# Regrouping a feature-major tile into pairs by way of DRAM, with eight key batches beside it and two linear maps multiplied into one

## What is computed

```python
def _encoder_block(x, Wq, bq, Wk, bk, Wv, bv, Wo, bo, rel_bias, W1, b1, W2, b2):
    q = x @ Wq.T + bq;  k = x @ Wk.T + bk;  v = x @ Wv.T + bv
    qm = q.reshape(d_batch * NB_HEADS, q_len, d_head)      # k and v likewise
    att = jax.nn.softmax(jnp.einsum('nqd,nkd->nqk', qm, km), axis=-1)
    ...                                                    # batch_pos from rel_bias
    att_out = jnp.einsum('nqk,nkd->nqd', att + batch_pos, vm)
    att_out = att_out.reshape(d_batch, q_len, d) @ Wo.T + bo
    att_block = layer_normalize(att_out + x)
    ff = (att_block @ W1.T + b1) @ W2.T + b2
    return layer_normalize(ff + att_block)
```

## Time and profile before

| | |
|---|---|
| median of 3 runs | 1202.9 us (1199.35 to 1207.03) |
| the profiled execution | 1196.92 us |
| its span, first to last instruction | 1195.0 us |
| mean granted TensorE clock | 0.964 of full speed |
| PE, DVE, ACT, POOL busy | 92%, 57%, 48%, 30% of the span |

### The profile page before, as it was taken

The page is one execution under the profiler, slowest core; times in us unless marked ns, Lnnn a source line. Parts: engine busy times, 40 slices in busy tenths (PEclk is TensorE's granted clock), DMA queues, the critical chain, the costliest instruction groups (busy, mean ns, idle before and its releaser), DMA issues.

```text
span 1195.0 us, 26831 instructions
## 1 busy us (share of the span) xinstructions
PE 1099.0 (92%) x9273; PEld 756.1 (63%) x9273; DVE 681.1 (57%) x2035; ACT 577.4 (48%) x1279; POOL 353.6 (30%) x554
## 2 busy tenths in 40 slices
PE   7879998999998899999988668899999999999987
PEld 4455666878776467566655446477777776666554
DVE  5575446455555564778865466533334334688774
ACT  5552224443343554677764133343534344678665
POOL 2217002112111304355440071040404040466561
PEclk9979999999999989999999759799999999999989
DMA  8700120122231003355540301011111211100000
GB/s 260 257 0 27 40 71 22 47 56 58 53 55 50 1 2 115 90 166 165 157 155 1 53 24 47 0 54 53 51 56 44 63 40 58 49 2 2 2 2 19
DMA packets 64859, 73.75 MB, mean 62 GB/s; under 512 B 5936, under 2 KB 57408, under 8 KB 64392
## 3 DMA queue, kind: packets, MB, share of 16 engines
q1 hardware_dynamic: 61496, 64.14, 19.5%
q0 software_dynamic: 1376, 7.49, 1.9%
q10 hardware_dynamic: 1904, 0.98, 0.5%
HBM read 69.98 MB, written 0.52 MB: 59 GB/s over the span
## 4 chain that ended last, share of the span: by engine, by line
PE 81%; DVE 7%; ACT 5%; DMA 3%; issue 2%; POOL 1%; ACTq 1%; SPq 0%; DVEq 0%; POOLq 0%
PE PS L544 14%; PE PS L556 13%; PE PS L1175 7%; PE PS L1186 6%; PE PS L831 5%; PE PS L795 4%; PE PS L547 3%; PE PS L838 2%; PE PS L1207 2%; PE PS L782 2%; PE PS L1164 2%; ACT XN L1419 2%; DMA AR<-AR 1%; PE PS L1157 1%; ACT AR L1419 1%
## 5 line engine op out<-in xcount | busy, mean ns | idle before, releaser
L556 PEld LDWEIGHTS PS<-WB,AR 128*128 128x128 f32 x1504 | 182.3, 192 | 42.8 <-issue 38.6
L556 PE MATMUL PS<-WB,AR 128*128 128x128 f32 x1504 | 182.9, 275 | 0.1
L1419 ACT ACTIVATE AR<-PS,WB 128x512 f32<-128x512 f32 x160 | 110.0, 687 | 148.8 <-PE PS L544 141.0
L2047 DVE SCALAR_TENSOR_TENSOR ACC<-PS,SM,ACC 128x128 f32<-128x128 f32 x192 | 54.1, 344 | 95.9 <-PE PS L556 94.5
L1922 DVE TENSOR_TENSOR AR<-PS,AR 128x512 f32<-128x512 f32 (+2 forms) x71 | 49.8, 701 | 92.4 <-issue 38.6
L544 PE MATMUL PS<-ZT,WB 128*128 128x512 f32 x208 | 100.5, 606 | 0.2 <-DMA WB<-in_units 0.2
L1175 PE MATMUL PS<-AR 64*128 64x257 f32 x512 | 90.5, 429 | 1.0 <-POOL AR L2882 1.0
L544 PE MATMUL PS<-XNT,WB 128*128 128x512 f32 x168 | 87.6, 628 | 0.6 <-DMA WB<-in_units 0.6
L1419 ACT ACTIVATE AR<-PS 128x512 f32<-128x512 f32 (+2 forms) x83 | 43.8, 528 | 85.2 <-PE PS L547 70.1
L1186 PE MATMUL PS<-W,AR 128*128 128x128 f32 x512 | 80.1, 282 | 1.3 <-ACT AR L1419 1.3
L2824 POOL TENSOR_TENSOR AR<-AR,SM 128x516 f32<-128x516 f32 x32 | 33.7, 1054 | 155.5 <-ACT SM L1419 93.8
(11 more groups left out here) (340 smaller groups left out, 2130.9 us busy)
## 6 DMA issues: line engine op xcount, KB each, us to landing
WB<-in_units SPq DMA_DIRECT2D x49, 385.0 KB, 3.1
CTX<-in_fside SPq DMA_DIRECT2D x32, 514.0 KB, 3.9
CTX<-in_ctxT SPq DMA_DIRECT2D x72, 130.0 KB, 2.1
CTX<-in_ctxN SPq DMA_DIRECT2D x32, 129.0 KB, 2.3
CTX<-in_ctxN SPq DMA_DIRECT2D x4, 516.0 KB, 7.0
AR<-in_ctxN SPq DMA_DIRECT2D x4, 516.0 KB, 10.6
AR<-in_ctxN SPq DMA_DIRECT2D x32, 64.5 KB, 3.1
AR<-in_l1x_w POOLq DMA_DIRECT2D x1, 2048.0 KB, 7.9
```

The lines of the kernel that those rows point to most:

```text
L556: m = pe.matmul(PS[:, 4 + hh, 128 * t:128 * t + 128], f_h[hh][:, c, 128 * t:128 * t + 128], WB[:, q, 2 * UNIT + 128 * c:2 * UNIT + 128 * c ...
L1419: return act.activation(o, i, fn, **k)
L2047: ins = dve.scalar_tensor_tensor(out=a, in0=y, scalar=f_w[:, 4 * hh + t, bass.ds(e, 1)], in1=a, op0=ALU.mult, op1=ALU.add)
```

## The change

The three tiles q, k and v are staged separately. Each is written to a DRAM buffer in its new partition order, as one DMA of 128 x 16 pieces of 64 elements (256 bytes), and read back as one DMA of 128 rows of 4 KB. All six DMAs are issued by SP. Queries and keys are waited for by `pair_landed`, values by `pair_v`.

`kv_early` has 8 batches in place of 12. The other 16 are divided: 10 before the output projection, 2 behind it and 4 behind the second map, where the six `keep_clock` matmuls are gone. ACT takes both keys and values of the last four.

After the landing POOL writes two of the four masked copies of the second half and ACT the other two; POOL's copies of v are gone, since PE reads v where it landed. PE does the first scores before it turns v. ACT runs exp(u+1) ahead of copy(u).

`W1` and `W2` are multiplied during `kv_early`, with `b1 @ W2` added to `b2`, and the sequence map, eviction, map becomes one map by the product, written over `l2a_w1`.

```diff
 LIVE = 8
+KV_EARLY = 8
...
+        dram = nc.dram_tensor("pair_dram", (3, P, TOK), F32, kind="Internal").ap()
+        pair_dram = [dram[k] for k in range(3)]
...
+        kv_order = [20 + n for n in range(12)] + [LIVE + n for n in range(12)]
...
-        c_v = ar(10240, TOK)
-        c_tokens = ar(2048, 3072)
-        c_pairs = ar(14336, 3072)
-        staged = lambda k: c_tokens.rearrange("p (u k x) -> p k u x", u=H, k=3)[:, k]
-        pair_part = lambda k: c_pairs.rearrange("p (c k m) -> p k m c", c=H, k=3)[:, k]
-
-        def to_pairs(u):
-
-
-            return (c_pairs[DK * u:DK * u + DK, :].rearrange("i (c y) -> i c y", c=H),
-                    c_tokens[:, 192 * u:192 * u + 192])
+        c_wide = ar(1024, P)
+        c_w1 = ar(1024 + P, P)
+        c_tokens = [ar(a, TOK) for a in (2048, 3072, 6144)]
+        c_pairs = [ar(14336 + TOK * k, TOK) for k in range(3)]
+        pair_part = lambda k: c_pairs[k].rearrange("p (c m) -> p m c", c=H)
+
+        def sent(k):
+
+            return (pair_dram[k].rearrange("(u i) (c x) -> (i c) u x", u=H, c=H),
+                    c_tokens[k].rearrange("p (u x) -> p u x", u=H))
+
+        def to_pairs(k):
+
+            return c_pairs[k], pair_dram[k]
...
+            sp.wait_ge(sig["pair_staged"], 1)
+            sp.dma_start(*sent(0)).then_inc(sig["pair_sent"], 16)
+            sp.wait_ge(sig["pair_staged_d"], 1)
+            sp.dma_start(*sent(1)).then_inc(sig["pair_sent_k"], 16)
+            sp.wait_ge(sig["pair_sent"], 16)
+            sp.dma_start(*to_pairs(0)).then_inc(sig["pair_landed"], 16)
             sp.wait_ge(sig["pair_staged"], 2)
-            sp.wait_ge(sig["pair_staged_d"], 1)
-            for u in range(1, H, 2):
-                sp.dma_start(*to_pairs(u)).then_inc(sig["pair_landed"], 16)
-            sp.wait_ge(sig["pair_landed"], 16 * H)
-            sp.wait_ge(sig["kv_ready"], 24)
+            sp.dma_start(*sent(2)).then_inc(sig["pair_sent"], 16)
+            sp.wait_ge(sig["pair_sent_k"], 16)
+            sp.dma_start(*to_pairs(1)).then_inc(sig["pair_landed"], 16)
+            sp.wait_ge(sig["pair_sent"], 32)
+            sp.dma_start(*to_pairs(2)).then_inc(sig["pair_v"], 16)
+            sp.wait_ge(sig["pair_landed"], 32)
+            sp.wait_ge(sig["pair_v"], 16)
+            sp.wait_ge(sig["kv_ready"], 2 * KV_EARLY)
...
-                pe.matmul(bank(k), VW[:, v, :], source, start=True, stop=True).then_inc(sig["cv_ready"], 1)
+                to = bank(k).rearrange("p (m c) -> p m c", c=H) if len(source.shape) == 3 else bank(k)
+                pe.matmul(to, VW[:, v, :], source, start=True, stop=True).then_inc(sig["cv_ready"], 1)
...
                 pe.wait_ge(sig["keys_landed0"], 32)
-                for n in range(12):
+                for n in range(KV_EARLY):
                     if n == 0:
                         pe.wait_ge(sig["pair_staged"], 1)
                     elif n == 1:
                         pe.wait_ge(sig["pair_staged_d"], 1)
+                        pe.transpose(PS[:, 1, 0:P], w("l2a_w1"), ident).then_inc(sig["lin_ready"], 1)
                     else:
                         pe.wait_ge(sig["kv_taken"], 2 * n - 2)
-                    kv_project(20 + n, 2 + 2 * (n % 2))
-
-            def kv_late():
-
-                pe.wait_ge(sig["keys_landed1"], 32)
-                pe.wait_ge(sig["keys_landed2"], 32)
-                for n in range(12):
-                    if 3 <= n < 9:
-                        pe.wait_ge(sig["kv_taken"], 24 + 2 * (n - 2))
-                    elif n >= 9:
-                        pe.wait_ge(sig["kv_taken"], 36 + n - 8)
-                        pe.wait_ge(sig["kv_taken_a"], n - 8)
-                    kv_project(8 + n, 2 * (n % 3))
+                    if n == 3:
+                        pe.matmul(PS[:, 1, P:2 * P], c_w1, w("l2a_w2"), start=True, stop=True)
+                        pe.matmul(PS[:, 1, 2 * P:3 * P], c_wide, w("l2a_w2"), start=True, stop=True)\
+                            .then_inc(sig["lin_ready"], 1)
+                    kv_project(kv_order[n], 2 + 2 * (n % 2))
+
+            def kv_late(first, last):
+
+                if first == 0:
+                    pe.wait_ge(sig["keys_landed1"], 32)
+                for m in range(first, last):
+                    if kv_order[KV_EARLY + m] == 15:
+                        pe.wait_ge(sig["keys_landed2"], 32)
+                    if m >= 3:
+                        d, a = kv_counts(m - 3 if m < 12 else m - 2)
+                        pe.wait_ge(sig["kv_taken"], d)
+                        if a:
+                            pe.wait_ge(sig["kv_taken_a"], a)
+                    kv_project(kv_order[KV_EARLY + m], kv_bank(m))
...
-                    pe.wait_ge(sig["pair_v"], half + 1)
-                    c_values(6 + half, 2, c_v[:, 512 * half:512 * half + 512])
-                taken("ck_taken", "ck_taken_d", "bias_taken_r")
-                pe.wait_ge(sig["kv_taken"], 24)
+                taken("ck_taken", "ck_taken_d")
+                pe.wait_ge(sig["kv_taken"], 2 * KV_EARLY)
                 c_scores(0, (0, 1), query)
                 c_scores(0, (2, 3), query)
-                taken("ck_taken_p", "pair_q")
+                pe.wait_ge(sig["pair_v"], 16)
+                for half in range(2):
+                    c_values(6 + half, 2, pair_part(2)[:, 32 * half:32 * half + 32, :])
+                taken("ck_taken", "ck_taken_p")
                 c_scores(1, (0, 1), query)
...
-            kv_late()
+            kv_late(0, 10)
             pe.wait_ge(sig["pair_out_landed"], 16 * 11)
             pe.wait_ge(sig["pair_out_pool"], 16 * (H - 11))
             project(ZT, w("l2a_o"))
+            kv_late(10, 12)
             turn(Z)
-            for hh in range(2):
-                half_taken(hh)
-                pe.matmul(bank(2 + hh), w("l2a_w1"), ZT[:, 512 * hh:512 * hh + 512], start=True, stop=True)\
-                    .then_inc(sig["lin_ready"], 1)
             pe.wait_ge(sig["acc_ready"], 2)
             carry(ACC)
+            project(ZT, w("l2a_w1"), half_taken)
+            kv_late(12, 16)
 
             def hidden(hh):
                 name = ("lin_taken", "lin_taken_d")[hh]
                 pe.wait_ge(sig[name], seen.up(name))
-            project(OT, w("l2a_w2"), hidden)
...
-                f(staged(k), PSF[:, TOK + TOK * k:2 * TOK + TOK * k].rearrange("p (u x) -> p u x", u=H),
-                  bias=col("l2a_b" + "qkv"[k])).then_inc(sig["pair_staged"], 1)
+                f(c_tokens[k], PSF[:, TOK + TOK * k:2 * TOK + TOK * k], bias=col("l2a_b" + "qkv"[k]))\
+                    .then_inc(sig["pair_staged"], 1)
                 act.wait_ge(sig["pair_staged"], seen.up("pair_staged"))
-            act.wait_ge(sig["pair_staged_d"], 1)
-            for u in range(0, H, 2):
-                act.dma_start(*to_pairs(u)).then_inc(sig["pair_landed"], 16)
             act.wait_ge(sig["bias_turned"], 1)
-            act.copy(c_rt, PS[:, 0, :]).then_inc(sig["bias_taken_r"], 1)
-            act.wait_ge(sig["bias_taken_r"], 1)
-            act.wait_ge(sig["pair_landed"], 16 * H)
+            act.copy(c_rt, PS[:, 0, :]).then_inc(sig["act_ran"], 1)
+            act.wait_ge(sig["act_ran"], seen.up("act_ran"))
+            seen.up("lin_ready", 2)
...
             dst = c_kb[:, 0:2048].rearrange("p (n h m c) -> p h n m c", n=16, h=4, m=2)
             of = pair_part(1)[:, 0:32, :].rearrange("p (n m) c -> p n m c", m=2)
             for h in (0, 1):
                 name = "ck_taken" if h else "act_ran"
                 f(dst[:, h], of, scale=w("mask4")[:, h:h + 1]).then_inc(sig[name], 1)
                 act.wait_ge(sig[name], seen.up(name))
-            act.copy(c_q[:, 512:1024].rearrange("p (m c) -> p m c", c=H), pair_part(0)[:, 32:64, :])                .then_inc(sig["pair_q"], 1)
-            act.wait_ge(sig["pair_q"], 1)
-            for u in range(8):
+            act.copy(c_q[:, 512:1024].rearrange("p (m c) -> p m c", c=H), pair_part(0)[:, 32:64, :])                .then_inc(sig["act_ran"], 1)
+            act.wait_ge(sig["act_ran"], seen.up("act_ran"))
+            dst = c_kb[:, 2048:4096].rearrange("p (n h m c) -> p h n m c", n=16, h=4, m=2)
...
+                act.wait_ge(sig[name], seen.up(name))
+            c_exp(0)
+            for u in range(1, 8):
                 c_exp(u)
-                c_turned(u)
-                if u == 4:
+                c_turned(u - 1)
+                if u == 5:
                     c_weighed(0)
                     c_sums(0)
+            c_turned(7)
             c_sums(1)
             c_weighed(1)
             act.wait_ge(sig["c_out"], 4)
             for u in range(0, 6):
                 act.dma_start(*to_tokens(u)).then_inc(sig["pair_out_landed"], 16)
             prepare(ACT.Sqrt)
-            for n in range(6, 12):
...
             norm(carried_tile, Z, 0.0)
+            for m in range(10, 12):
+                kv_take(m)
             turned(ZT[:, :])
```

(42 more changed lines are left out.)

45 lines of the change are left out of this document (31 added, 14 removed).

## The result

Timed beside each other, the changed kernel takes 1181.4 us (median of 4 runs, 1177.7 to 1187.9) and the kernel before 1203.9 us (1199.4 to 1207.0): a ratio of 0.984, 95% interval 0.980 to 0.988. That is 22.5 us less; 1187, or 16.1 us less, had been forecast. The same changed kernel was timed twice more, at 0.982 (0.977 to 0.988) and 0.984 (0.980 to 0.988) of the kernel before.

What follows compares the result with a forecast made beforehand. The prediction took the stage to be bound by the wait for the pairs to land, then a queue behind POOL. Gains of 8.1 + 7.2 + 0.8 = 16.1 us from the median 1202.9 gave 1187 us, range 1178 to 1203.

Steps and rivals of the forecast that it cites:

- term 2: From landing of q and k to the late batches: 36.3 us against 43.5, 7.2 us gained.
- term 3: After the stage: fewer batches before the output projection, later evictions and merged maps, together 0.8 us gained.
- Term 1, the move: Staging to landing through DRAM in six DMAs: q and k landed at 680.5 against 688.6, 8.1 us gained.
- d: Time of one 256-byte piece on its DMA engine in the move: taken as 34 ns, floor 19, ceiling 116.
- The cover holds: Before the landing: eight early batches end about 672, merged-map work adds under 1 us, still before 674.7.
- the busiest engine of this stretch: From landing to late batches: DVE was claimed to be the busiest engine.
- The strided read of v: PE's products of v, read with a stride: cost taken as zero, with +3.8 us kept for the range.
- The rival of a clock that stays low: Through the stage PE stays at the low clock, landing to late batches gains about nothing: 1195 us, chance 0.15.
- Two batches fewer: Before the output projection: ten batches instead of twelve, 1.8 us gained.
- Merged maps: Behind the stage: merging is worth nothing, since the carry into PSUM waits for DVE's addition.
- The copy into ZT: Behind the stage: two key evictions stand ahead of it on DVE, with 0.49 us of slack, costing 0.5 us.
- The rival of doubled writes: In the move small writes cost double, 68 ns: landing 693.5, 4.9 us lost there, 1200 us in all, chance 0.18.

Runs made afterwards that it cites:

- x7: Changed kernel with k's read from DRAM issued before v's write: 1177.1 us, 0.985 of the kernel before.
- x6: Changed kernel with q, k and v written to DRAM as contiguous 4 KB rows, outputs not the reference's: 1183.3 us, 0.986 of the kernel before.
- x0: The changed kernel again, unchanged, timed and profiled a second time: 1178.4 us, 0.982 of the kernel before.
- x2: Changed kernel with ScalarE's old order, each exp followed by the copy of its own block: 1190.1 us, 0.992 of the kernel before.
- x8: Changed kernel with filler matmuls between the early key batches and the first scores: 1179.9 us, 0.983 of the kernel before.
- x9: x8 with the products reading v in runs of 32 neighbouring values and writing PSUM with a stride: 1179.6 us, 0.983 of the kernel before.
- x10: Changed kernel with filler ahead of the first scores, v read in runs of 32, and filler ahead of the carry: 1180.5 us, 0.982 of the kernel before.
- x4: Changed kernel with filler matmuls between the transposes of Z and the carry of ACC: 1179.8 us, 0.986 of the kernel before.
- x11: The changed kernel again, unchanged, timed and profiled a third time: 1184.3 us, 0.984 of the kernel before.
- x3: Changed kernel with the two linear maps in sequence again instead of merged: 1186.2 us, 0.991 of the kernel before.

## Why the prediction was right, and where its sizes were off

The forecast was "faster", by the mechanism it named, and the time lies in its range. With 19 ns in place of 34 its sum would have been 21.9 us and the time 1181.0, against 1181.4 measured. That this comes so close is partly luck: term 2 gave 1.3 to 2.1 us less than forecast by the table and term 3 gave 0.3 to 1.6 more, and the kernel before has one profile. By the table (before against the three changed profiles) the terms came out so:

**Term 1, the move: 8.1 us forecast, 14.4 to 14.6 measured.** The step at fault is the choice of d: 34 ns was taken, "the right size, its dearer reading, because the target is new"; 19.2 ns was measured, the other reading of the same pair. The formula was near: with 19 ns it had given 674.7, and q and k landed at 673.3. It counted all of v's write ahead of k's read, 2.5 us at 19.2 ns; x7 shows that v's write costs 0.5 to 1.5 us there. Why the pieces took 34 ns in the first row of the pair stays open. It is not that the window was partly empty: share x window x 16 / packets is the mean time of the packets themselves, and in the profile after the writes' first 464 packets, with a share of 27.1% in 661 to 663, took 18.7 ns each. "The cover holds" was true by 0.78 us, DVE's wait before its copy: x6 and x7 show that a landing 1 us earlier meets a busy DVE. The move has thus given about what it can unless the early batches shrink too.

**Term 2, landing to late batches: 7.2 us forecast, 6.0 measured in TensorE's rows** (43.5 to 37.5) **and 5.1 to 5.9 by the table.** DVE was not "the busiest engine of this stretch": from 688.6 to 732.1 it was busy for 25.9 us and TensorE for 30.4. The sum held all the same, since it was built from DVE's waits. First maximum at 5.1 us after the landing (5.3 forecast); waits for v 2.09 and 1.00 us (2.1 and 1.2); last wait 4.46 (4.13). The one step missed is the exp wait that stayed, 1.31 us in the profile after and 0.73 in x0. x2 confirms the main cause: about 6 us hang on ScalarE's order.

**The strided read of v was put at zero, and that was right for a reason not given.** Both kernels run these products at the lower clock, where the packed operand took 3.78 us and the strided one 3.79. At the high clock the stride costs 1.5 us of TensorE's work (x8 against x9), of which 0.4 us or nothing came through in elapsed time (3.73 us against 3.36 in x9 and 4.12 in x10). A price read at one clock was carried to the other; it cost nothing only because the clock was low here.

**The rival of a clock that stays low did not come about.** The clock was low from 676 to 682 and 691 to 696, and 0.98 from 696 to 710, where the earlier trace rows had 0.50 from 700 to 712. x9 and x10 (35.9 and 36.2 us from landing to late batches) put a price on what is left, the stride with it: 2 to 3 us against the changed kernel's 38.3 to 39.1, but only 1.0 to 1.3 against x4's 37.2.

**Term 3, behind the stage: 0.8 us forecast, 1.1 to 2.4 measured**, a right sum of wrong parts. Two batches fewer: forecast 1.8, measured 0.0 (ZT late) or 1.8 (x0, x11). Merged maps "worth nothing": so x3 shows, but the forecast had no term for TensorE's idle stretch ahead of the carry, which now takes 3.4 to 3.8 us at the lower clock instead of 1.98; a loss of 1.4 to 2.6 us that x4 gives back. The removed `keep_clock` matmuls, which "did not hold the clock", stood behind the carry and have no part in it. The copy into ZT costs 0.3 us where 0.5 was put. Against that, the stretch to the experts is 2.2 to 3.6 us shorter; the low clock comes earlier and ends earlier (741 to 750 against the earlier trace rows's 764 to 777). That the clock makes the difference is argued from this and from x8 (0.50 from 749 to 761, 35.6 us) and x10 (1.00 from 749 to 761, 30.8 us); no run tests it.

**The rival of doubled writes** had the right rule and the wrong base: x6 shows a factor of 1.9 between pieces and whole rows, but 68 ns was the doubling of a number that was itself too high.

## What to carry to other kernels

Where two rows price the same small DMA piece differently, carry both through the sum and say what each gives: here the dearer one, a mean of 101 packets, cost 5.8 us, and the cheaper one was right. Before shortening a transfer, look at what the engines that wait for it have queued: here 0.8 us of DVE's idle time was all that was left to win. Where TensorE runs at its lower clock, costs hide (a strided operand), and where it idles ahead of a step on the critical path, the next matmuls can cost nearly double (the carry, 3.4 to 3.8 us instead of 1.98): look at the granted clock of both sides of every gap that an edit opens. Before reading a gain from the stretches of one profile, look at how far the stretches that the edit doesn't touch differ from those of the same kernel.

## What the runs showed of the hardware

- Writing 512 KB from SBUF to DRAM in pieces of 256 bytes: 19.2 ns a piece and engine, 214 GB/s, 5.1 us from issue to landing; in rows of 4 KB 163 ns a row, 404 GB/s, 3.0 us.
- Two matmuls of 128x512 in float32 (four records) whose moving operand has a stride of 256 bytes take 3.80 us at a granted clock of 1.00 (x8) and 3.79 us at 0.50 (x0). Read in runs of 32 values and written to PSUM with a stride of 64 bytes, they take 2.3 us of work at 1.00 (x9, x10).
- TensorE's 13 stops put down to `issue` from the landing to the late batches in five profiles end 2.3 to 3.0 us after a 16 KB transfer on the queue of instructions has started.
- A DVE copy of 128x512 between places of SBUF took 0.59 us when it began ahead of GpSimd's masks, 1.48 us when it began 0.08 us behind them with a transfer under way (x7), and 0.78 us when it began 1.6 us behind them (x6).
